# Parts for twelve last quarters, two more banks in the first block, w1's upper parts on GpSimd, routing on logits

## Time and profile before

| what | value |
|---|---|
| runs | 491.46 us median of 3 (491.3 to 491.7) |
| the profiled execution | 491.48 us, of which the span is 489.6 |
| TensorE busy | 477.3 us (97%), granted clock 1.0 all through |
| VectorE, ScalarE, GpSimd busy | 367.5, 338.0, 240.8 us |
| DMA | mean 91 GB/s, 44.59 MB |

### The profile page before, as it was taken

One profiled execution on the slowest core, in us unless ns is written; L12 is line 12 of the kernel. 1 busy time (PEld: TensorE's weight loads), 2 busy tenths in 40 slices (PEclk: granted clock), 3 DMA queues, 4 the chain that ended last, 5 costly groups with the idle time before them and its releaser, 6 DMA issues.

```text
span 489.6 us, 6291 instructions
## 1 busy us (share of the span) xinstructions
PE 477.3 (97%) x1873; PEld 302.0 (62%) x1873; DVE 367.5 (75%) x714; ACT 338.0 (69%) x569; POOL 240.8 (49%) x252
## 2 busy tenths in 40 slices
PE   8999999999999999999999999999999999999996
PEld 4676776566557556555755755565566565777775
DVE  3889877759975895997496799935669994667644
ACT  3776787677757668773857767646778765687874
POOL 3235632627875162886516268834616874321322
PEclk9999999999999999999999999999999999999999
DMA  7771121058410017730003555111046611003200
GB/s 252 233 269 33 54 64 41 7 154 234 129 43 1 1 44 208 204 106 1 1 2 129 150 175 151 44 64 43 1 120 182 195 43 44 0 1 117 79 1 21
DMA packets 21297, 44.59 MB, mean 91 GB/s; under 512 B 3856, under 2 KB 4240, under 8 KB 21264
## 3 DMA queue, kind: packets, MB, share of 16 engines
q1 hardware_dynamic: 14928, 32.66, 21.5%
q10 hardware_dynamic: 6336, 11.54, 8.3%
HBM read 40.91 MB, written 3.28 MB: 90 GB/s over the span
## 4 chain that ended last, share of the span: by engine, by line
PE 58%; issue 16%; POOL 11%; DVE 10%; ACT 3%; DMA 1%; POOLq 0%; ACTq 0%; DVEq 0%
PE Y L377 12%; PE U L346 8%; PE U L350 7%; PE U L347 7%; POOL qs L955 5%; PE Y L368 4%; PE Y L373 4%; PE Y L370 4%; POOL xT L929 4%; DVE hid_lo L773 2%; PE A L450 2%; PE A L442 1%; POOL pool_a L961 1%; PE A L436 1%; DVE gy L782 1%
## 5 line engine op out<-in xcount | busy, mean ns | idle before, releaser
L929 POOL TENSOR_TENSOR xT<-xT,gy 128x512 f32<-128x512 f32 x63 | 84.3, 1338 | 146.2 <-DVE gy L782 146.0
L346 PE MATMUL U<-xhi,w1lo 128*128 128x512 f32 x256 | 151.6, 592 | 3.0 <-ACT hid_hi L575 1.2
L377 PE MATMUL Y<-hid,w 128*128 128x512 f32 x264 | 134.2, 589 | 0.0
L773 DVE TENSOR_TENSOR hid_lo<-hid,hid_hi 128x512 fp32r<-128x512 f32 x124 | 97.8, 793 | 39.0 <-ACT hid_hi L575 38.5
L577 ACT ACTIVATE hid<-U,small 128x512 f32<-128x512 f32 x132 | 90.6, 689 | 48.6 <-PE U L350 46.2
L574 ACT ACTIVATE hid<-U,small 128x512 f32<-128x512 f32 x124 | 85.5, 690 | 43.8 <-PE U L350 39.3
L350 PE MATMUL U<-xlo,w1hi 128*128 128x512 f32 x256 | 100.8, 394 | 0.0
L347 PE MATMUL U<-xhi,w1hi 128*128 128x512 f32 x256 | 100.5, 392 | 0.0
L955 POOL TENSOR_TENSOR qs<-q,pool_a 128x512 f32<-128x512 f32 x64 | 80.1, 1251 | 15.0 <-DVE pool_a L830 14.8
L346 PEld LDWEIGHTS U<-xhi,w1lo 128*128 128x128 f32 x256 | 48.1, 188 | 62.1 <-issue 35.9
L575 ACT ACTIVATE hid_hi<-U,small 128x512 fp32r<-128x512 f32 x124 | 84.8, 684 | 0.0
(11 more groups left out here) (135 smaller groups left out, 515.9 us busy)
## 6 DMA issues: line engine op xcount, KB each, us to landing
G<-gate_dram SPq DMA_DIRECT2D x32, 512.0 KB, 4.3
vb<-v_dram ACTq DMA_DIRECT2D x44, 256.0 KB, 3.6
vb<-v_dram SPq DMA_DIRECT2D x20, 256.0 KB, 4.5
pool_a<-wexp_dram SPq DMA_DIRECT2D x8, 256.0 KB, 6.8
w<-wexp_dram SPq DMA_DIRECT2D x8, 256.0 KB, 6.8
v_dram<-v SPq DMA_DIRECT2D x8, 256.0 KB, 2.2
xnt<-xtok_dram SPq DMA_DIRECT2D x4, 256.0 KB, 5.1
xT<-xT_dram SPq DMA_DIRECT2D x4, 256.0 KB, 7.1
```

The source lines that it names most:

```text
L346: mm(dst, w1lo[:, e, f, :], xhi[:, k % NB, :], start=True, stop=False)
L377: last = mm(dst, w2[:, g % E, f, :], hid[:, n % HS, cut], start=first, stop=final)
L773: dve.tensor_tensor(hid_lo[:, c, :], hid[:, n % HS, :], hid_hi[:, c, :], ALU.subtract).then_inc(h_lo, 1)
L929: pool.tensor_tensor(xT[:, h, b, :], xT[:, h, b, :], gy[:, g % 2, :], ALU.add).then_inc(acc, 1)
```

## The change

It touches six places.

- `in_parts`: twelve last quarters (QUIET) are made in parts too. ScalarE makes only hid for them, VectorE copies it to hid_hi and then makes hid_lo; TensorE waits for both before the first matmul. Three more first quarters (112, 144, 192) are made directly. 133 quarters are in parts after it. w2hi and w2lo hold all four quarters; GpSimd makes the last ones for two experts at a time in slots 33, 37, 39 and 41.
- hid_hi and hid_lo have four buffers in place of three.
- Experts 2 and 3 of the first block sum up in A[1] and A[2] (free until the first attention unit), so the first combines are needed later, and come in slots 13 and 14 in place of 10 and 11.
- The upper parts of w1 for experts 2 to 7 are made by GpSimd, in slots 0, 4, 8, 12, 16 and 20, in front of its split of w2, not by VectorE.
- Routing finds the two largest logits instead of the two largest probabilities, and divides the exponentials of the two by their sum, 17 linked instructions in place of 20, in nine steps. Block 1 spreads them over nine slots (14 to 22) in place of five.
- A scratch area for dynamic DMAs is made smaller, which gives room for the larger tiles.

```diff
@@ -29,7 +29,7 @@
 HS, QS, SS = 5, 8, 4
-FP, PS, GS, VS = 3, 3, 6, 5
+FP, PS, GS, VS = 3, 4, 6, 5
@@ -42,6 +42,8 @@
+ROUTE = 9
@@ -64,15 +66,14 @@
+def route_slots(k):
+
+    return {1: 9, 2: 5, 3: 5}.get(k, 3)
-    if not 0 <= t < route_slots(k):
-        return ()
-    return (t + 1,) if route_slots(k) == 5 else ((1, 2), (3, 4), (5,))[t]
-
-def route_slots(k):
-    return 5 if k in (1, 2, 3) else 3
+    return [1 + n for n in range(ROUTE) if n * route_slots(k) // ROUTE == t]
@@ -116,16 +117,23 @@
-    return 4 * g + {0: 10}.get(g, 7)
-
-LATE = (slot_of(2, T_PO) + 1, slot_of(2, T_PO) + 5)
+    return 4 * g + {0: 13, 1: 10}.get(g, 7)
+
+LATE = (112, 144, 164, 168, 192)
+LAST_PARTS = (33, 37, 39, 41)
+QUIET = (51, 83, 123, 167, 171, 215, 219, 235, 239, 243, 247, 251)
+
+def by_vector(n):
+
+    return n % FC == FP and n in QUIET
     scans = any(slot_of(i, T_SC) - 3 <= n < slot_of(i, T_PO if i == UNITS - 1 else T_OUT) for i in range(UNITS))
-    return n >= FC and n % FC < (1 if scans else FP) and n not in LATE
+    return n >= FC and n % FC < (1 if scans else FP) and n not in LATE or by_vector(n)
@@ -168,8 +176,8 @@
         gate_T = sb("gate_T", [P, NB, 32])
-        w2hi = sb("w2hi", [P, E, FP, P], F32R)
-        w2lo = sb("w2lo", [P, E, FP, P], F32R)
+        w2hi = sb("w2hi", [P, E, FC, P], F32R)
+        w2lo = sb("w2lo", [P, E, FC, P], F32R)
@@ -196,6 +204,10 @@
+
+        def rows_of(g):
+
+            return A[g - 1] if g in (2, 3) else Y[g % 2]
@@ -353,10 +365,10 @@
                     pe.wait_ge(w2_in[g], 16)
-                if f == 0 and g >= 2:
-                    pe.wait_ge(comb, g - 1)
+                if f == 0 and g >= 4:
+                    pe.wait_ge(comb, g - 1 if g >= 6 else g - 3)
                 first, final = f == 0, f == FC - 1
-                halves = [(Y[g % 2][:, :], slice(0, NT))]
+                halves = [(rows_of(g)[:, :], slice(0, NT))]
@@ -364,6 +376,9 @@
                         pe.wait_ge(w2lo_s, g)
+                    if f == FP:
+                        pe.wait_ge(w2lo_s, E + g % E // 2 + 1)
+                        pe.wait_ge(h_lo, parts_to(n + 1))
@@ -567,7 +582,7 @@
                 bias = w(W_B1 + n % (E * FC), 1)
-                if in_parts(n):
+                if in_parts(n) and not by_vector(n):
@@ -680,9 +695,6 @@
             def split_w1(e):
-                if e >= 2:
-                    dve.wait_ge(w1_in[e], 16)
-                    dve.tensor_copy(w1hi[:, e].rearrange("p f n -> p (f n)"), w1raw[:, e, :]).then_inc(w1hi_s, 1)
@@ -736,32 +748,35 @@
                 if step == 1:
+                    dve.wait_ge(lg_sub, k + 1)
+                    link(dve.scalar_tensor_tensor(out=flat(m(3)), in0=flat(m(0)), scalar=0.0, in1=flat(tie4),
+                                                  op0=ALU.is_equal, op1=ALU.mult))
+                    link(dve.tensor_reduce(r(5), m(3), AX.X, ALU.max))
+                if step == 2:
+                    link(dve.tensor_tensor(m(4), tie4, bc(r(5)), ALU.is_equal))
+                    link(dve.scalar_tensor_tensor(out=flat(m(6)), in0=flat(m(4)), scalar=-1e30, in1=flat(m(0)),
+                                                  op0=ALU.mult, op1=ALU.add))
+                if step == 3:
+                    link(dve.tensor_reduce(r(4), m(6), AX.X, ALU.max))
+                    link(dve.tensor_tensor(m(3), m(6), bc(r(4)), ALU.is_equal))
+                if step == 4:
+                    link(dve.tensor_tensor(m(3), m(3), tie4, ALU.mult))
+                    link(dve.tensor_reduce(r(5), m(3), AX.X, ALU.max))
+                if step == 5:
+                    link(dve.tensor_tensor(m(5), tie4, bc(r(5)), ALU.is_equal))
+                    link(dve.tensor_tensor(m(7), m(4), m(5), ALU.add))
+                if step == 6:
                     link(dve.tensor_reduce(r(1), m(1), AX.X, ALU.add))
-                    link(dve.reciprocal(r(2), r(1)))
-                    link(dve.tensor_tensor(m(2), m(1), bc(r(2)), ALU.mult))
-                    link(dve.tensor_reduce(r(3), m(2), AX.X, ALU.max))
-                if step == 2:
-                    link(dve.tensor_tensor(m(3), m(2), bc(r(3)), ALU.is_equal))
-                    link(dve.tensor_tensor(m(3), m(3), tie4, ALU.mult))
-                    link(dve.tensor_reduce(r(5), m(3), AX.X, ALU.max))
-                    link(dve.tensor_tensor(m(4), tie4, bc(r(5)), ALU.is_equal))
-                if step == 3:
-                    link(dve.scalar_tensor_tensor(out=flat(m(6)), in0=flat(m(4)), scalar=-2.0, in1=flat(m(2)),
-                                                  op0=ALU.mult, op1=ALU.add))
-                    link(dve.tensor_reduce(r(4), m(6), AX.X, ALU.max))
-                    link(dve.tensor_tensor(m(3), m(6), bc(r(4)), ALU.is_equal))
-                    link(dve.tensor_tensor(m(3), m(3), tie4, ALU.mult))
-                if step == 4:
-                    link(dve.tensor_reduce(r(5), m(3), AX.X, ALU.max))
-                    link(dve.tensor_tensor(m(5), tie4, bc(r(5)), ALU.is_equal))
-                    link(dve.tensor_tensor(m(7), m(4), m(5), ALU.add))
-                    link(dve.scalar_tensor_tensor(out=flat(m(3)), in0=flat(m(7)), scalar=0.5, in1=flat(m(2)),
+                    link(dve.tensor_tensor(m(3), m(7), m(1), ALU.mult))
+                if step == 7:
+                    link(dve.tensor_reduce(r(3), m(3), AX.X, ALU.add))
+                    link(dve.scalar_tensor_tensor(out=r(6), in0=r(1), scalar=1e-9, in1=r(3), op0=ALU.mult, op1=ALU.add))
+                if step == 8:
+                    link(dve.reciprocal(r(7), r(6)))
+                if step == 9:
+                    link(dve.scalar_tensor_tensor(out=gate[:, b].rearrange("p e t -> p t e"), in0=m(3), scalar=0.5, in1=bc(r(7)),
                                                   op0=ALU.mult, op1=ALU.mult))
-                if step == 5:
-                    link(dve.scalar_tensor_tensor(out=r(6), in0=r(3), scalar=1e-9, in1=r(4), op0=ALU.add, op1=ALU.add))
-                    link(dve.reciprocal(r(7), r(6)))
-                    link(dve.tensor_tensor(gate[:, b].rearrange("p e t -> p t e"), m(3), bc(r(7)), ALU.mult))
@@ -770,6 +785,9 @@
                     dve.wait_ge(h_f, n + 1)
+                    if by_vector(n):
+                        dve.wait_ge(down, PARTS[PARTS.index(n) - PS] + 1)
+                        link(dve.tensor_copy(hid_hi[:, c, :], hid[:, n % HS, :]))
@@ -779,7 +797,7 @@
                     dve.wait_ge(acc, g - 1)
-                dve.scalar_tensor_tensor(out=gy[:, g % 2, :], in0=Y[g % 2][:, :], scalar=w(W_B2 + e, 1),
+                dve.scalar_tensor_tensor(out=gy[:, g % 2, :], in0=rows_of(g)[:, :], scalar=w(W_B2 + e, 1),
@@ -787,6 +805,7 @@
                 dve.wait_ge(acc, g)
+                dve.wait_ge(g_in[g % GS // EQ], 16 * (g // GS + 1))
@@ -933,15 +952,30 @@
+            def w1_upper(e):
+                pool.wait_ge(w1_in[e], 16)
+                if e == 2:
+                    pool.wait_ge(w1hi_s, 2)
+                pool.tensor_copy(w1hi[:, e].rearrange("p f n -> p (f n)"), w1raw[:, e, :]).then_inc(w1hi_s, 1)
                 pool.wait_ge(w2_in[e], 16)
-                pool.tensor_copy(w2hi[:, e].rearrange("p f n -> p (f n)"),
+                pool.tensor_copy(w2hi[:, e, 0:FP].rearrange("p f n -> p (f n)"),
                 pool.wait_ge(w2hi_s, done)
-                pool.tensor_tensor(w2lo[:, e].rearrange("p f n -> p (f n)"), w2[:, e, 0:FP].rearrange("p f n -> p (f n)"),
-                                   w2hi[:, e].rearrange("p f n -> p (f n)"), ALU.subtract).then_inc(w2lo_s, 1)
+                pool.tensor_tensor(w2lo[:, e, 0:FP].rearrange("p f n -> p (f n)"),
+                                   w2[:, e, 0:FP].rearrange("p f n -> p (f n)"),
+                                   w2hi[:, e, 0:FP].rearrange("p f n -> p (f n)"), ALU.subtract).then_inc(w2lo_s, 1)
+
+            def split_w2_last(e):
+
+                done = E + e // 2 + 1
+                pool.tensor_copy(w2hi[:, e:e + 2, FP], w2[:, e:e + 2, FP]).then_inc(w2hi_s, 1)
+                pool.wait_ge(w2hi_s, done)
+                pool.tensor_tensor(w2lo[:, e:e + 2, FP], w2[:, e:e + 2, FP], w2hi[:, e:e + 2, FP],
+                                   ALU.subtract).then_inc(w2lo_s, 1)
@@ -1001,8 +1035,12 @@
                     add_y(due[n])
+                if n % 4 == 0 and n // 4 + 2 < E:
+                    w1_upper(n // 4 + 2)
                     split_w2((n // 4 + 1) % E)
+                if n in LAST_PARTS:
+                    split_w2_last(2 * LAST_PARTS.index(n))
@@ -1073,7 +1111,7 @@
     arrays = lay_out(inputs)
-    nc = bacc.Bacc("TRN2", target_bir_lowering=False, num_devices=1)
+    nc = bacc.Bacc("TRN2", target_bir_lowering=False, num_devices=1, dynamic_dma_scratch_size=1024)
     gates = [nc.dram_tensor(f"gate_dram{s}", (NB * E * 4, P), F32).ap() for s in range(4)]

```

## The result

The changed kernel takes 489.56 us (median of 5, 489.2 to 490.0) against 491.46 us: ratio 0.9965, 95% interval 0.9954 to 0.9976. 489.7 was forecast. The profiled execution has a span of 487.7 us in place of 489.6.

The account below looks back on a forecast made before the run. TensorE was taken to bound the kernel, busy 477.3 of 489.6 us. From 491.48 us: -1.4 (quarters), -1.3 (scan start), +0.6 (first block), +0.3 (late w2 split) gave 489.7 us, range 486.3 to 492.9.

Parts of the forecast that it names:

- Quarters: TensorE's slots: twelve last quarters into parts, three first quarters out, net nine at 0.16 us each, -1.4 us.
- The slack: The twelve quarters: copy and subtraction, even held 1.31 us by a GpSimd add, take 3.1 us of 4.2 available.
- Rival 3: The twelve quarters do not pay: eight in the last blocks meet GpSimd's adds and give back 0.16 each; 491.0 us, chance 0.15.
- Scan start: Slots 144 and 145, start of the third scan: shorter routing and direct quarter 144 remove nearly all 1.60 us, -1.3 us.
- the sign: Slots 144 and 145 would last near 1.55 us if the forecast was right, as long as before if wrong.
- First block: Block 0, casts to GpSimd and later combines: between -2.2 and +3.5 us, taken as +0.6.
- The later stretch: First block from slot 13: delayed combines and GpSimd's adds meet VectorE's work; from -1.6 to +2.5 us.
- the walk: Stepping through both queues in the first block, GpSimd winning every meeting: 3 us more VectorE waiting in slots 14 to 17.
- the early stretch: First block, early: six GpSimd instructions from 12.1 us hold VectorE's routing of block 0; from -0.6 to +1.0 us.
- The split of w2's last quarters: GpSimd's split in slots 33, 37, 39 and 41 may hold VectorE: bounds 0 and +1.2 us, taken as +0.3.
- Rival 1: The relief comes through: waits of slots 11, 19 and 20 go, -1.6 at the scan; 486.3 us, chance 0.25.
- Rival 2: GpSimd holds VectorE up in slots 1 to 8 and 13 to 24: block 0 +3.5, late split +1.2; 493.5 us, chance 0.2.

Follow-up runs that it names:

- e3: The changed kernel without the twelve last quarters in parts and without GpSimd's split of w2's last quarters: 491.09 us, ratio 0.9999 to the kernel before.
- e7: The changed kernel with the routing of before (20 linked instructions, five slots for blocks 1 to 3): 491.13 us, ratio 0.9996 to the kernel before.
- e4: The changed kernel with first quarters 112, 144 and 192 in parts again: 491.06 us, ratio 0.9996 to the kernel before.
- e1: The changed kernel with w1's upper parts of experts 2 to 7 made by VectorE again: 488.94 us, ratio 0.9953 to the kernel before.
- e2: The changed kernel with the first block's first two combines back in slots 10 and 11, the two more banks kept: 487.67 us, ratio 0.9926 to the kernel before.
- e9: e2 with w1's lower parts of experts 2 to 7 made one slot earlier by VectorE: 486.55 us, ratio 0.9901 to the kernel before.
- e8: The kernel before with only first quarters 112, 144 and 192 made directly: 489.83 us, ratio 0.9968 to the kernel before.
- e11: e9 with three more quarters, 140, 156 and 184, made directly: 484.78 us, ratio 0.9870 to the kernel before.

## Why the prediction was right, and where it was not

**Quarters: right.** -1.4 us was the term; the slots give 1.87 less 0.37, so -1.5, and e3 the 1.87 again. The slack held: L790, VectorE's copy, takes 414 to 919 ns, so it did meet GpSimd, and none of the twelve slots waits for it. Rival 3 falls.

**Scan start: right, one size off.** Slots 144 and 145 gave 1.06 us of the 1.3, and stayed 0.3 and 0.2 above the 1.55 that was named as the sign. The split between the causes was as put: e7 gives 0.47 of slot 144 to the routing, e4 gives 0.60 of slot 145 to quarter 144.

**First block: the mechanism was right, the size was not.** +0.6 was the term. By the table it is +0.4 and +1.2 less the 0.3 of slot 2, so +1.3, well inside the bounds of -2.2 and +3.5. The later stretch went as in the walk: adds into slots 13 to 15, hid_lo, routing and w1lo held one after the other, waits in slots 19 and 23. w1lo of expert 5 was ready at 42.0 us (43.1 in the walk). In the early stretch the mis-sized step was "the routing ends about 1.9 us later than 17.53": it ended at 17.86 us, which is 0.3 later, or 0.7 counted from the start of slot 0. The walk had each of GpSimd's six instructions hold one of VectorE's; four were held, by 0.3 to 0.5 us each; the reductions, and the products that fell between GpSimd's instructions, took their usual 0.19. Slots 10 and 12 grew by 0.67 and 0.41 us, and slot 11 gave 0.70 back with the bank's wait: +0.4.

Which item costs what was not split in the prediction, and e1's expectation split it wrongly. The late combines cost 1.9 us (e2). The casts cost some 0.6 us (e1, whose interval overlaps the changed kernel's): by the traces 1.1 in slots 10 and 12 and 0.5 in slot 37, where other changes gave it back as well, less 0.6 in slots 13 to 23 (the profiled execution of e1 was 0.5 us below its median, so the traces show more than the medians). The new routing, from which the prediction took six instructions (1.2 us) out of the later stretch, saves 2.1 us by the start of slot 32 (e7).

**The split of w2's last quarters:** +0.3 was taken, slot 37 shows 0.44 and slot 47 gives 0.30 back; e1, e7 and e9 lose slot 37's part with the split in place, so it isn't the split's own.

**The step that failed** is the sentence "All other waits in TensorE's queue are small, or part of the attention's own chain, which the change leaves alone". Slots 118 and 206 held waits of 0.5 and 0.8 us (slot 206's before the last reduction of the scan, as the row shows). They are of the attention's own chain, and the change did not leave it alone: quarters 112 and 192, costed at their 0.16 us alone, took a hid_lo each out of VectorE's queue and removed the waits: e4 and e8. The routing made slots 133 and 189 1.2 us longer, which e7 takes back. Both terms were missing, -1.4 and +1.2, and they nearly cancel. The block was 0.7 us worse than the term, and 0.39 us of the 1.97 in the traces lie before slot 0 starts and are not the change's. So the total is as near as 0.1 us partly by luck; the parts were off by up to 1.4 us.

Rival 1 fails as stated: the waits of slots 11 and 20 went, but that of slot 19 grew, and slots 10, 12 and 23 got longer. Rival 2's mechanism is shown by the rows and by e2, at 1.3 us and not 3.5. The instructions that were held took 1.27 to 1.78 us where 0.19 to 0.69 are usual, and the price is nearly the rest of the GpSimd instruction that runs. The Trainium skill (GPSIMD Engine Reference, 8. Key points) has GpSimd share its SBUF interfaces with VectorE and contend with VectorE instructions that have two SBUF inputs; these rows agree (1.78 against 0.69 us).

Open: how much of e7's 1.6 us comes from fewer routing instructions and how much from the spread, and what the move of the casts is worth by itself beyond the overlap of the intervals.

## What to carry to other kernels

A resource that lets work be done later is no reason to do it later: ask in which slots the in-order engine has room, and put the work there (e2, e9). Before changing a unit of work that runs beside a dependent chain, follow the chain to the next place where the bound engine waits for it; there it may cost three to five times what it saves in the engine's own queue (e8, e11). When work moves between VectorE and GpSimd, count the moved instruction against both queues (e1: 1.1 us lost in two slots, 0.6 gained in eleven others).

## What was not expected of the hardware

- A VectorE instruction with two SBUF inputs that starts while GpSimd runs an elementwise instruction on 256 to 512 columns waits for nearly all that is left of it. In the changed kernel's trace 36 hid_lo start with over 0.13 us of one left, and each takes its usual 0.69 us plus what was left of the GpSimd instruction less 0.14 to 0.15 us: 1.78 us at 32.70, where 1.23 us of the add were left. The 69 that meet nothing on GpSimd take 0.65 to 0.69. GpSimd's power of 16 columns (L1008, 2.89 us) and its reciprocal root of 4 (L953, 1.02 to 1.39 us) do not hold it: seven hid_lo start inside one and none takes over 0.69 us. VectorE and then GpSimd of the changed kernel from 329 us on:

```profile
329.41 0.43 DVE L790 CAST hid_hi<-hid 128x512 fp32r<-128x512 f32 x1 [0.16 <-ACT hid L592]
329.88 0.69 DVE L791 TENSOR_TENSOR hid_lo<-hid,hid_hi 128x512 fp32r<-128x512 f32 x1
```

```profile
329.02 2.89 POOL L1008 TENSOR_TENSOR quk<-quk,half 128x16 f32<-128x16 f32 x1
```

Copy and subtraction take their usual 0.43 and 0.69 us, both inside the 2.89 us of L1008.
- The holding up goes both ways. A cast of 128x512 from float32 to float32r takes GpSimd 0.61 us (VectorE 0.42), but 1.13 us at 11.82, where VectorE's w1lo had begun at 11.80. The add at 32.26 takes 1.67 in place of 1.27 to 1.29, behind the w1lo that ran from 32.10 to 32.78, and then holds the hid_lo at 32.70: whichever begins first holds the other.
